# A cross attention in which TensorE takes the last three tiles of a unit in one step instead of two

## The chip, the cores and the metric

The kernel runs on one core of a Trainium2 chip. The metric is the time of one execution on the device, in microseconds (us). The kernel before took 3461.85 us, the median of three runs that lie between 3461.8 and 3472.22 us.

The core's engines each work through a program of their own and meet at semaphores: TensorE (PE in the profile, with its weight loads as PEld), VectorE (DVE), ScalarE (ACT), GpSimd (POOL) and SyncE (SP, which starts the DMAs).

## The reference, cut to what matters

The whole computation is a two-layer network over x (32 batches of 64 rows of 128) with a context of 32 x 1601 x 128: an attention with its feed-forward, a linear attention, a mixture of experts, a second cross attention, a rotary attention and a second mixture. The change touches the second cross attention alone:

```
def _L1_xattn_ref(x, context, mask, Wq, Wkv, Wout, b_out):
    HEADS = 16
    DIM_HEAD = 64
    SCALE = DIM_HEAD ** (-0.5)
    ...
    q = x @ Wq.T
    kv = context @ Wkv.T
    k, v = jnp.split(kv, 2, axis=-1)
    ...
    sim = jnp.einsum('bhid,bhjd->bhij', q, k) * SCALE
    max_neg = -jnp.finfo(sim.dtype).max
    sim = jnp.where(mask[:, None, None, :], sim, max_neg)
    attn = jax.nn.softmax(sim, axis=-1)
    out = jnp.einsum('bhij,bhjd->bhid', attn, v)
    out = out.transpose(0, 2, 1, 3).reshape(B, Nq, HEADS * DIM_HEAD)
    return out @ Wout.T + b_out
...
x = x + _L1_xattn_ref(_layernorm(x, axis=-1), ctx_1024, mask_BxS2_bf1, L1_xattn_Wq, L1_xattn_Wkv, L1_xattn_Wout, L1_xattn_b_out)
```

The kernel folds the weights: query and key weights of a head are one 128 x 128 matrix, and so are value and output weights. Scores are then folded queries against the raw context, and the probabilities mix the raw context before the folded value weights project it.

## The kernel before

The stage is `cross_attention_1` (from L2089). A unit `v` is half the heads (8) of one batch, 64 units in all, so a unit has 8 heads x 64 queries = 512 columns. Its context is cut into `KT` = 13 tiles of 128 rows (`kt` = 0 to 12). A tile `n` = 13 v + kt goes through these steps:

- `scores(n)` on PE (L2210): three bf16 matmuls 128x512 (L2221 to L2223) into one of three PSUM banks;
- `copy` on ACT (L2434) adds the mask and writes the scores to SBUF, `running_max` on DVE (L2336) follows it;
- `shift` on DVE (L2353) subtracts the maximum and `exp` on ACT (L2441) takes the exponential, both for two tiles at once, the last tile of a unit alone; POOL adds up the probabilities (L2179 to L2188);
- `mix(n)` on PE (L2241): context tile times probabilities, f32 128x512, which the chip runs as two MATMULs of L2248, accumulated over the 13 tiles of the unit.

`scores` runs `LEAD` = 22 tiles ahead of `mix`. Between them PE does small work, which `between(n)` (L2298) places by `kt`: `denominators` of the unit before at kt 1 (L2255), `project` at kt 3 (L2264), `turn_peaks` at kt 5 (L2229), `spread_shift` at kt 8 (L2237), `queries` and `final`.

- `queries` (L2268, matmuls at L2271) makes the folded queries of a later pair of batches, a quarter of the heads at a time. The table `QUERIES` = {(0, 10): 0, (1, 10): 1, (2, 9): 2, (2, 11): 3} gives the places as (v mod 4, kt); this runs while v // 4 + 1 < 16.
- `final` (L2274, matmul at L2277) stacks the result of a finished batch. It runs at kt 12 of every even unit after the first.

All of these small works write the same PSUM bank, `R_SMALL` = 7. `take_small` (L2204) makes each wait until the one before it has been read out: for `final` behind `queries` that is the semaphore `q_low`, and it is reached only when ACT has copied the bank (`queries` of act, L2448) and DVE has then subtracted (`queries` of dve, L2379). ACT and DVE have their place in their own programs for this, by the same (v mod 4, kt), behind the copy and the running maximum of tile n + 22.

The order of PE's work is written out by hand in the loop at L2313: for each unit, for each entry of `tile_pairs` (tiles 0-1, 2-3, 4-5, 6-7, 8-9, 10-11, and 12 alone), all `scores(n + 22)` of the step, then `between(n)` for each of its tiles, then all `mix(n)`. The loops of DVE (L2408) and ACT (L2462) go tile by tile and are not touched by the change.

Of the kernel before, what the change touches and what calls it, by code (L numbers as in the profile page):

```python
# [35 lines left out]
KT = -(-S // P)  # L36
# [2052 lines left out]
def cross_attention_1(c):  # L2089
# [51 lines left out]
    tile_pairs = [(j, 2 * j, min(2 * j + 2, KT)) for j in range(NP)]  # L2141
# [59 lines left out]
    def pe(eng):  # L2201
# [8 lines left out]
        def scores(n):  # L2210
            v, kt = n // KT, n % KT
            bt, b, half = v // 2, v // 2 % 2, v % 2
            if kt == 0:
                eng.wait_ge(q_low, bt // 2 * 4 + 2 * half + 2)
                eng.wait_ge(ctx_split, SPLIT * bt + SPLIT)
            wait_if(eng, copied, n - SB + 1)
            q = slice(half * QU, half * QU + QU)
            w = slice(kt * P, kt * P + P)
            o = c.ps[:, n % SB, 0:QU]
            i = bt // 2 % 2  # L2220
            eng.matmul(o, ch[:, b, w], qh[:, i, b, q], start=True, stop=False)  # L2221
            eng.matmul(o, ch[:, b, w], ql[:, i, b, q], start=False, stop=False)  # L2222
            eng.matmul(o, cl[:, b, w], qh[:, i, b, q], start=False, stop=True).then_inc(scored, 1)  # L2223
# [17 lines left out]
        def mix(n):  # L2241
            v, kt = n // KT, n % KT
            b = v // 2 % 2
            if kt == 0:
                eng.wait_ge(ctx_loaded[b], (v // 4 + 1) * 32)
                wait_if(eng, u_made, v - 1)
            eng.wait_ge(exps, v * NP + kt // 2 + 1)
            eng.matmul(c.ps[:, R_MIX + v % 2, :], ctxn[:, b, kt * D:(kt + 1) * D], st[:, v % 2, kt, :],  # L2248
                       start=kt == 0, stop=kt == KT - 1).then_inc(mixed, 1)
# [24 lines left out]
        def final(bt):  # L2274
            b = bt % 2
            take_small((out_made, bt + 1))
            mm = eng.matmul(c.ps[b * L:(b + 1) * L, R_SMALL, 0:D], c.C("stack"), acc[:, b, :], start=True, stop=True)  # L2277
            mm.then_inc(f_ps, 1)
# [19 lines left out]
        def between(n):  # L2298
            v, kt = n // KT, n % KT
            if kt == 1 and v > 0:  # L2300
                denominators(v - 1)
            if kt == 3 and v > 0:
                project(v - 1)
            if kt == 5 and v + 1 < UNITS:
                turn_peaks(v + 1)
            if kt == 8 and v + 1 < UNITS:
                spread_shift(v + 1)
            if (v % 4, kt) in QUERIES and v // 4 + 1 < PAIRS:
                queries(v // 4 + 1, QUERIES[v % 4, kt])
            if kt == 12 and v > 0 and v % 2 == 0:  # L2310
                final(v // 2 - 1)

        for v in range(UNITS + 1):  # L2313
            for j, a, z in tile_pairs:
                tiles = range(v * KT + a, v * KT + z)
                for n in tiles:
                    if n + LEAD < TILES:
                        scores(n + LEAD)
                for n in tiles:
                    between(n)  # L2320
                for n in tiles:
                    if n < TILES:
                        mix(n)
# [103 lines left out]
    def act(eng):  # L2427
# [34 lines left out]
        for n in range(TILES + KT):  # L2462
# [8 lines left out]
            if a < TILES and a % KT % 2 == 0:  # L2471
                exp(a // KT, a % KT // 2)

    m.engines = dict(sp=sp, pool=pool, pe=pe, dve=dve, act=act)
    m.after = [(out_made, B)]
    return m
# [482 lines left out]
```

## Time and profile before

| | |
|---|---|
| median of three runs | 3461.85 us |
| profiled execution, its time | 3466.28 us |
| its span, first to last instruction | 3464.4 us |
| outside the span | 1.88 us |
| granted TensorE clock, mean of the span | 0.967 |
| the stage of the change | about 1352 to 2905 us of the span |
| busy share of the span: PE, DVE, ACT, POOL | 95%, 69%, 55%, 46% |

The profile is one execution. A row of the timeline gives the start in us from the span's start, the duration, the engine, the line of the kernel, the operation with what it writes and reads, and in brackets the idle time of the engine ahead of it with what ended it. The recorded duration of a matmul includes a modelled end, so 0.38 us of a bf16 128x512 matmul is not its share of the stream: for that one reads the distance of starts. Rows that merge several instructions (x4) run to the end of the last. A few matmul records are missing from the trace (in the timeline a start is then skipped).

### The profile page before, as it was taken

To read this page: it belongs to the slowest core of one execution; us is meant where nothing else is said; L and a number is where in the kernel's file an instruction comes from. 1 tells how busy PE (TensorE), PEld (TensorE's weight loads), DVE (VectorE), ACT (ScalarE), POOL (GpSimd) and SP (SyncE) were. 2 spreads that over 40 slices of the span, in tenths; PEclk is the share of its full clock that TensorE was granted. 3 is DMA by queue.
4 is the path that set the end of the run, shared out by engine and by line. 5 is a ranking of instruction groups with operands and counts; after the bars stand their busy time and mean duration, and the time that the engine had idled before them with its cause. 6 is when DMAs were issued, how large, how long until landed. Compare 5 with 4: busy or idle time off the path is not lost. (4 is left out here: it accounts for less than half of the span.)

```text
span 3464.4 us, 67377 instructions
## 1 busy us (share of the span) xinstructions
PE 3283.1 (95%) x26253; PEld 1902.2 (55%) x26385; DVE 2391.5 (69%) x5437; ACT 1904.4 (55%) x2600; POOL 1609.5 (46%) x1271
## 2 busy tenths in 40 slices
PE   7799999999997898999999999999999997979998
PEld 4566666666665775455445555545554544655555
DVE  7877777777784435777777777777777775653333
ACT  5466666666664234666666666666666663432222
POOL 5433333333322102777777777777777764310000
PEclk7899999999999699999999999999999999979999
DMA  1133333333320002011110111101111000010000
GB/s 74 32 73 76 75 75 83 73 73 75 76 50 1 26 1 73 20 39 39 39 39 20 39 39 39 39 20 39 39 39 39 21 28 1 1 77 1 1 1 13
DMA packets 90493, 138.92 MB, mean 40 GB/s; under 512 B 14464, under 2 KB 67776, under 8 KB 89408
## 3 DMA queue, kind: packets, MB, share of 16 engines
q1 hardware_dynamic: 90176, 134.61, 14.3%
q8 instruction: 210, 3.44, 0.4%
q14 instruction: 107, 0.88, 0.1%
HBM read 94.15 MB, written 1.05 MB: 27 GB/s over the span
## 5 line engine op out<-in xcount | busy, mean ns | idle before, releaser
L2434 ACT ACTIVATE arena<-banks,arena 128x512 f32<-128x512 f32 x832 | 560.3, 687 | 477.4 <-PE banks L2223 477.4
L2248 PE MATMUL banks<-arena 128*128 128x512 f32 x1664 | 803.9, 603 | 0.8 <-ACT arena L2441 0.8
L2182 POOL TENSOR_TENSOR arena<-arena 128x1024 f32<-128x1024 f32 x256 | 603.9, 2359 | 165.7 <-ACT arena L2441 164.6
L1220 DVE TENSOR_REDUCE arena<-banks 128x1 f32<-128x512 f32 (+1 forms) x896 | 529.4, 627 | 166.6 <-PE banks L1056 162.3
L2336 DVE TENSOR_TENSOR banks<-arena,banks 128x512 f32<-128x512 f32 x640 | 444.2, 694 | 242.7 <-ACT arena L2434 223.1
L1357 ACT ACTIVATE arena<-banks 128x1024 f32<-128x1024 f32 (+1 forms) x448 | 423.7, 961 | 306.5 <-PE banks L1137 303.9
L2353 DVE TENSOR_TENSOR arena<-arena,banks 128x1024 f32<-128x1024 f32 (+1 forms) x448 | 507.1, 1133 | 1.6 <-PE banks L2238 1.2
L2441 ACT ACTIVATE arena<-arena 128x1024 f32<-128x1024 f32 (+1 forms) x448 | 443.0, 989 | 11.1 <-DVE arena L2353 10.9
L2248 PEld LDWEIGHTS banks<-arena 128*128 128x128 f32 x1664 | 290.0, 190 | 220.8 <-issue 200.1
L2223 PE MATMUL banks<-arena 128*128 128x512 bf16 x830 | 313.2, 377 | 2.5
L2222 PE MATMUL banks<-arena 128*128 128x512 bf16 x786 | 297.9, 379 | 4.1
L981 POOL TENSOR_TENSOR arena<-arena,one 128x512 bf16<-128x512 f32 x124 | 105.7, 852 | 400.5 <-ACT arena L1321 400.5
L1157 PE MATMUL banks<-arena 128*32 128x192 f32 (+1 forms) x6656 | 288.8, 279 | 2.2 <-ACT arena L1357 2.1
L2221 PE MATMUL banks<-arena 128*128 128x512 bf16 x754 | 285.4, 378 | 0.1
L1157 PEld LDWEIGHTS banks<-arena 128*32 128x32 f32 x6656 | 184.7, 109 | 154.0 <-ACT arena L1357 71.8
L2179 POOL TENSOR_TENSOR arena<-arena 128x1024 f32<-128x1024 f32 x64 | 151.3, 2365 | 229.6 <-ACT arena L2441 229.4
L2010 DVE SCALAR_TENSOR_TENSOR arena<-banks,weights,arena 128x512 f32<-128x512 f32 x128 | 95.9, 750 | 220.2 <-PE banks L1872 128.3
L1930 ACT ACTIVATE arena<-banks,weights 128x512 f32<-128x512 f32 x128 | 88.0, 687 | 260.8 <-PE banks L1862 260.8
L1056 PE MATMUL banks<-arena 64*128 64x512 bf16 x768 | 182.4, 383 | 31.2 <-DVE arena L1220 28.9
L1872 PEld LDWEIGHTS banks<-arena 128*128 128x128 f32 x1536 | 179.6, 193 | 44.8 <-issue 35.2
L1872 PE MATMUL banks<-arena 128*128 128x128 f32 x1536 | 186.6, 279 | 1.8 <-DVE arena L2010 1.7
L2222 PEld LDWEIGHTS banks<-arena 128*128 128x128 bf16 x832 | 81.1, 97 | 191.2 <-issue 144.1
(353 smaller groups left out, 5159.4 us busy)
## 6 DMA issues: line engine op xcount, KB each, us to landing
arena<-arena SPq DMA_DIRECT2D x768, 50.0 KB, 2.2
arena<-in_ctxT SPq DMA_DIRECT2D x32, 800.5 KB, 6.2
arena<-in_ctx SPq DMA_DIRECT2D x32, 768.0 KB
fold<-in_ctxT SPq DMA_DIRECT2D x16, 800.5 KB, 4.6
foldv<-in_ctxT SPq DMA_DIRECT2D x16, 800.5 KB, 5.0
arena<-in_m2w SPq DMA_DIRECT2D x3, 2048.0 KB, 13.3
arena<-in_xw SPq DMA_DIRECT2D x1, 2048.0 KB, 7.9
weights<-in_weights SPq DMA_DIRECT2D x1, 1920.0 KB, 12.3
```

Of the source, the lines that this page charges most:

```text
L1157: mm = eng.matmul(c.ps[HR * x:HR * x + HR, 6, a:z], v9[0:w, b, e:e + HR], pr[0:w, at % 4, rt * 512 + t2 * 256 + a:rt * 512 + t2 * 256 + z] ...
L1220: eng.tensor_reduce(o, s, AX, ALU.max).then_inc(a_max, 1)
L1357: eng.activation(pr[0:w, at % 4, :].rearrange("p (x n) -> p x n", x=2)[:, :, 0:n], c.ps[0:w, bank:bank + 2, 0:n], ACT.Exp, scale=scale).th ...
L1872: mm = eng.matmul(c.ps[:, 4 + e % 2, j * P:(j + 1) * P], hT[:, (g * units + u) % NH, j * P:(j + 1) * P], w3[:, wo * D:(wo + 1) * D], start ...
L2182: eng.tensor_tensor(part, part, tiles, ALU.add).then_inc(sums, 1)
L2222: eng.matmul(o, ch[:, b, w], ql[:, i, b, q], start=False, stop=False)
L2223: eng.matmul(o, cl[:, b, w], qh[:, i, b, q], start=False, stop=True).then_inc(scored, 1)
L2248: eng.matmul(c.ps[:, R_MIX + v % 2, :], ctxn[:, b, kt * D:(kt + 1) * D], st[:, v % 2, kt, :], start=kt == 0, stop=kt == KT - 1).then_inc(m ...
L2336: eng.tensor_tensor(peak if kt == KT - 1 else c.ps[:, R_MAX, :], st[:, v % 2, kt, :], so_far, ALU.max)\
L2353: eng.tensor_tensor(tiles, tiles, c.ps[:, R_SHIFT, :].unsqueeze(1).to_broadcast([P, z - a, QU]), ALU.subtract)\
L2434: eng.activation(st[:, v % 2, kt, :], c.ps[:, n % SB, :], ACT.Identity, bias=hide[:, kt, v // 2:v // 2 + 1])\
L2441: eng.activation(tiles, tiles, ACT.Exp, scale=scale).then_inc(exps, 1)
```

## The change

Tiles 10, 11 and 12 of a unit become one step of PE's loop. The steps up to tile 9 stay as they were. No instruction is added or taken away; the number of tiles in a step is all that changes, and with it the order in which PE issues the same work.

```diff
             if kt == 12 and v > 0 and v % 2 == 0:
                 final(v // 2 - 1)
 
+        steps = [(a, z) for _, a, z in tile_pairs[:-2]] + [(KT - 3, KT)]
         for v in range(UNITS + 1):
-            for j, a, z in tile_pairs:
+            for a, z in steps:
                 tiles = range(v * KT + a, v * KT + z)
                 for n in tiles:
                     if n + LEAD < TILES:
```

Written out, PE's order at the end of a unit is:

```
before: scores(10+22) scores(11+22)  between(10) between(11)  mix(10) mix(11)
        scores(12+22)  between(12)  mix(12)
after:  scores(10+22) scores(11+22) scores(12+22)
        between(10) between(11) between(12)  mix(10) mix(11) mix(12)
```

## Rows read from the trace of the kernel before

**Rows 1.** The page, busy time and its share of the span for each engine.
```profile
PE 3283.1 (95%) x26253; PEld 1902.2 (55%) x26385; DVE 2391.5 (69%) x5437; ACT 1904.4 (55%) x2600; POOL 1609.5 (46%) x1271
```

**Rows 2.** Busy us of each engine in two stretches of four units, granted clock (PEclk), DMA.
```profile
1400.00:1496.00 96.00, 95.52 (x432) 48.34 (x440) 74.38 (x115) 63.47 (x90) 71.14 (x45) 1.00 0.11 35
...
2739.00:2835.00 96.00, 95.57 (x434) 48.29 (x441) 74.20 (x115) 63.01 (x89) 69.33 (x43) 1.00 0.09 26
```

**Rows 3.** PE by line, 1400 to 2860 us: busy us, mean ns, then idle before.
```profile
L2248 PE MATMUL banks<-arena 128*128 128x512 f32 x1583 | 766.2, 603 | 0.0
```

**Rows 4.** Waits, 1400 to 2860 us: us in total, times, longest us.
```profile
ACT arena L2434 <- PE banks L2223: 465.3, 395, 2.0
...
PEld banks L2229 <- DVE arena L2373: 28.5, 61, 0.8
...
PEld banks L2277 <- DVE arena L2379: 6.4, 15, 0.4
PEld banks L2277 <- issue: 6.4, 15, 0.4
```

**Rows 5.** Timeline of PE, a step of two tiles without small work.
```profile
1821.05 0.38 PE L2221 MATMUL banks<-arena 128*128 128x512 bf16 x1
...
1822.34 1.88 PE L2248 MATMUL banks<-arena 128*128 128x512 f32 x4
1824.06 0.38 PE L2221 MATMUL banks<-arena 128*128 128x512 bf16 x1
```

**Rows 6.** Timeline of PE, tiles 10 to 12 of unit 18.
```profile
1828.46 0.38 PE L2221 MATMUL banks<-arena 128*128 128x512 bf16 x1
...
1829.76 1.05 PE L2271 MATMUL banks<-xT,fold 128*128 128x128 f32 x8
1830.65 1.88 PE L2248 MATMUL banks<-arena 128*128 128x512 f32 x4
1832.37 0.38 PE L2221 MATMUL banks<-arena 128*128 128x512 bf16 x1
...
1833.11 0.43 PE L2277 MATMUL banks<-arena,consts 128*64 128x128 f32 x2
...
1834.44 0.38 PE L2221 MATMUL banks<-arena 128*128 128x512 bf16 x1
```

**Rows 7.** Timeline of ACT and DVE, the same stretch of unit 18.
```profile
1831.41 0.60 ACT L2448 ACTIVATE arena<-banks 128x512 bf16<-128x512 f32 x1
...
1831.77 0.69 DVE L2336 TENSOR_TENSOR banks<-arena,banks 128x512 f32<-128x512 f32 x1
...
1832.37 0.68 DVE L2379 TENSOR_TENSOR arena<-banks,arena 128x512 bf16<-128x512 f32 x1
```

**Rows 8.** Timeline of PE, tiles 10 to 12 of unit 16.
```profile
1779.60 0.38 PE L2221 MATMUL banks<-arena 128*128 128x512 bf16 x1
...
1780.89 1.05 PE L2271 MATMUL banks<-xT,fold 128*128 128x128 f32 x8
...
1784.24 0.43 PE L2277 MATMUL banks<-arena,consts 128*64 128x128 f32 x2
...
1785.57 0.38 PE L2221 MATMUL banks<-arena 128*128 128x512 bf16 x1
```

**Rows 9.** Timeline of ACT and DVE, the same stretch of unit 16.
```profile
1781.98 0.60 ACT L2448 ACTIVATE arena<-banks 128x512 bf16<-128x512 f32 x1 [0.85 <-PE banks L2271]
...
1782.62 0.69 DVE L2379 TENSOR_TENSOR arena<-banks,arena 128x512 bf16<-128x512 f32 x1 [0.75 <-ACT arena L2448]
```

**Rows 10.** Busy us of each engine in stretches around lower clocks, granted clock as above.
```profile
1000.00:1050.00 50.00, 46.05 (x830) 30.20 (x818) 36.82 (x84) 30.01 (x36) 5.06 (x9) 0.97 0.14 27
...
2895.00:2898.00 3.00, 1.25 (x4) 0.28 (x2) 0.00 (x0) 0.60 (x1) 2.57 (x3) 1.00 0.00 0
...
2901.00:2904.00 3.00, 0.71 (x3) 0.34 (x3) 1.20 (x5) 0.00 (x0) 0.06 (x1) 0.58 0.00 0
```

**Rows 11.** Timeline of PE, at the end of the stage.
```profile
2897.94 1.02 PE L2255 MATMUL banks<-one,arena 128*128 128x1 f32 x8 [1.75 <-POOL arena L2188]
```

## The prediction

> **What bounds the kernel now.** Start with the busy shares of the page. PE is busy for 95% of the span and no other engine above 69% [rows 1]. Then take the stage of the change alone, by stretches of four units: in 96 us PE is busy for 95.5, at the full clock of 2.4 GHz (granted 1.00), DVE for 74 and ACT for 63 [rows 2]. The grouping by line says the same: ahead of 1583 matmuls of `mix` PE was idle for 0.0 us [rows 3]. The list of waits shows the others waiting for PE, ACT for 465.3 us before its copies [rows 4]. So in this stage time is PE's stream: work of PE that is only reordered costs nothing, and every us in which PE stands still is a us of the kernel, since no later slack of PE can take it back.
>
> The distance of starts gives the stream's prices. In a step of two tiles without small work, six score matmuls take 1822.34 - 1821.05 = 1.29 us, so one tile of scores 0.645, and four MATMULs of `mix` take 1824.06 - 1822.34 = 1.72 us, 0.86 a tile [rows 5].
>
> **What the change takes away.** One alternation between scores (bf16) and mixes (f32) per unit, 64 in all. I take its price as nothing: the step of rows 5 is 3.01 us for two tiles, and a single-tile step at the same rates would be 1.505 us. Nothing in that step is left over for a turn. The largest turn I can find is at small work: `final` starts 0.31 us after the last score matmul (1832.80 from the even spacing behind 1832.37, then 1833.11) where 0.215 is the spacing [rows 6]. Charged to all 64 units, 0.1 us would be 6 us of gain. That is one end; the other is zero, and rows 5 are the nearer case, because the alternation that goes is one without small work.
>
> **What it moves.** The three scores of a step need three free banks. Scores of tile 12 + 22 wait for the copy of tile 9 + 22, issued a step earlier; 1.72 us of mixes and 1.29 us of scores lie between. ACT's copy takes less than 0.7 us, and ACT is the one who waits [rows 4]. Cost nothing. Mixes of tiles 10 to 12 need exponentials that ACT makes before its copy of tile 10 + 22, or right behind tile 9's. Cost nothing. The next unit's scores start 2.58 us of mixes behind the last ones; again the copies are done. No DMA and nothing of POOL's program is touched or passed.
>
> The small work is another matter. `queries` and `final` use one bank, and `final` waits until ACT and DVE have emptied it. Before, two mixes and one tile of scores lay between them: 1.72 + 0.645 = 2.36 us of PE's own work. After, nothing lies between them where both fall into tiles 10 to 12. Behind the waiting `final` on PE stand the mixes of 10, 11 and 12 and everything after; they are ready and can't pass. The table of places gives two such cases.
>
> Case A, `queries` at kt 11 (v mod 4 = 2, v = 2 to 58): 15 times. In unit 18 the last query matmul ends at 1829.76 + 1.05 = 1830.81, ACT's copy runs from 1831.41 to 1832.01, DVE's running maximum to 1832.46, DVE's subtraction from 1832.37 to 1833.05, and `final` starts at 1833.11, 0.06 us later [rows 6, 7]. The whole cover is used up already: the waits name L2379 as what was last before 15 of the 30 `final`s, though the 0.4 us there are no longer than at the 15 that name only issue, so nothing is lost yet [rows 4]. After the change queries end 0.645 later, at 1831.46, so ACT can copy from 1831.50 to 1832.10; DVE was busy until 1832.46 with its running maximum in either order, so the subtraction stays where it is and `final` starts at 1833.11 as before. But PE has by then not done mixes 10 and 11. Everything after is late by just those: 1.72 us. 15 x 1.72 = 25.8 us.
>
> Case B, `queries` at kt 10 (v mod 4 = 0, v = 4 to 56; unit 0 has no `final`): 14 times. In unit 16 queries end at 1780.89 + 1.05 = 1781.94; ACT starts its copy at 1781.98, 0.04 later, and DVE ends at 1782.62 + 0.69 = 1783.31 [rows 8, 9]. Both engines waited for this, so the chain moves with it: 0.645 later, to 1783.95, and `final` starts at 1784.01 instead of 1784.24. It comes 0.23 us earlier with 1.72 us of mixes still to do: 1.72 - 0.23 = 1.49 us late. 14 x 1.49 = 20.9 us.
>
> The other units: v mod 4 = 1 has `queries` at kt 10 and no `final`; v mod 4 = 3 has neither; units 60 and 62 have a `final` and no `queries`. Cost nothing, with one doubt. In v mod 4 = 1 ACT and DVE get their query work 0.645 us later and do what is queued behind it later (exponential, copies, shift, running maxima). `turn_peaks` of the next unit already waits for DVE's projection (28.5 us over 61 times, 0.47 on average against the 0.42 that a turn shows at `final`, longest 0.8) [rows 4]. If the lag reached it, it could cost up to 0.8 - 0.47 = 0.3 us in 16 units, 5 us. DVE has over 20 us of idle in 96 to take it up [rows 2], so I take zero.
>
> **The sum.** 25.8 + 20.9 = 46.7 us longer. Against the profiled execution: span 3464.4 + 46.7 = 3511.1, with the 1.88 us outside it 3513.0 for an execution that took 3466.28. The median lies 4.43 us below that execution, so 3461.85 + 46.7 = 3508.5 us.
>
> **A rule against a row: the clock.** While the clock is granted in full here, PE will now stand still for up to 1.8 us at a time, 29 times. The trace has such a gap at the end of this stage: PE was idle for 1.75 us after dense mixes [rows 11], with 1.25 of 3 us busy, and the granted clock of that stretch stayed at 1.00; it fell to 0.58 (part of it at 1.2 GHz) only in 2901 to 2904, after small matmuls and a second gap, with 0.71 of 3 us busy [rows 10]. In the new gaps dense work stands directly on both sides. I take no loss. The Trainium skill ("TensorE: Matmul & The Clock Gate", the section "Why this matters for your kernels") warns that idle gaps between bursts of matmuls send the clock back to its lower level. By that rule the time is that of rival 1; the trace agrees with it for the second gap, not for the first.
>
> The Trainium skill ("Perfetto Trace Analysis", section "Matmul Optimizations") also asks that matmuls execute back-to-back in batches, which would speak for larger steps. The stretches of this stage are at 1.00 already [rows 2], so by this trace a larger batch has nothing to win.
>
> **The rivals.**
> 1. The stalls are there and the clock falls in many of them. In the stretch 1000 to 1050 the clock fell once, and the mean of 0.97 makes that (1 - 0.97) x 50 = 1.5 us [rows 10]. In all 29 stalls that is 44 us, 3552; in half of them 3530. Against it speak rows 10 and 11. Chance 0.07.
> 2. Faster: the alternation has a price that starts don't show, and the bank is free sooner than I say, because DVE takes the query work ahead of its other work. This decides if the stalls together stay under 6 us, 0.2 us each. Then 3461.85 - 6 + 0 to 6 = 3456 to 3462. Against it: DVE's order is fixed, and with nothing queued ahead the chain from the last query matmul to the end of L2379 is still 1.36 us [rows 8, 9]. Chance 0.02.
> 3. The stalls are longer than the chain, or a second wait follows them. In case B ACT has, behind the query copy, an exponential and the copies of tiles 11 + 22 and 12 + 22 still to do, which before were partly done by then. After the stall PE has 3 x 0.86 us of mixes and 0.645 of scores ahead of the first scores that need the second of these copies, 3.2 us, against some 0.7 + 1.0 + 0.7 us on ACT. Should 0.5 us be missing each time, it is 29 x 0.5 = 14.5 us more, 3523. Chance 0.05.
> 4. The change does nothing, since PE does other work in the wait. There is none: PE's order is fixed. Chance 0.01.
>
> **How the numbers follow.** The forecast, stalls of case A and B at full clock, has 0.85, at 3508.5. Its own bounds are - 6 (alternations) and + 5 (lag at `turn_peaks`), and about 4 us either way for the spread of the medians: 3498.5 to 3517.5. To hold 8 in 10 nothing more is needed, but a few falls of the clock (5 x 1.5) belong in: 3498 to 3524. A measurement of this kernel can tell about 0.3%, 10.4 us, from no change. Faster 0.02 (rival 2 in part), same 0.03, slower 0.95.
>
> **What would show each step right or wrong.** In the profile after, L2277 (one line lower) should show an idle time of some 1.6 to 2.1 us before it, ended by L2379's counterpart, in 29 places, together near 50 us; PE's busy time in a stretch of four units stays 95.5 while the stretch takes 99.2 us instead of 96.0 (two stalls). The granted clock stays 1.00 there. `mix` and scores show no other waits. Wrong if the idle time ahead of `final` is well under 1.3 us, if the clock falls behind it, or if waits appear at `scores`, `mix` or `turn_peaks`.

## The result and the profile after

The changed kernel takes 3517.43 us, the median of four runs (3509.99 to 3524.8), against 3467.03 us for four runs of the kernel before beside it: a ratio of 1.0143, 95% interval 1.0114 to 1.0172. Its profiled execution has a span of 3511.5 us, where the kernel before had 3464.4. Line numbers behind the change are one higher (ACT's copy is L2435, its query copy L2449, DVE's running maximum L2337, its subtraction L2380); on PE `mix` stays L2248, `queries` L2271, `final` L2277.

The page of the kernel after, engines:

```profile
PE 3297.0 (94%) x26385; PEld 1908.2 (54%) x26385; DVE 2393.3 (68%) x5437; ACT 1901.7 (54%) x2600; POOL 1611.7 (46%) x1271
```

Busy us of each engine over four units, twice, granted clock, DMA (answers to [rows 2]):

```profile
1500.00:1599.20 99.20, 96.14 (x441) 48.60 (x441) 74.31 (x114) 62.81 (x89) 70.63 (x44) 1.00 0.11 34
1699.00:1798.20 99.20, 96.14 (x441) 48.54 (x440) 74.36 (x115) 62.82 (x89) 70.64 (x44) 1.00 0.11 34
```

Every engine does the work it did, in a longer time. (PE's busy time is 0.6 us above [rows 2] because this trace has all 441 matmul records and that one 432.) The clock is still granted in full. Four units take 99.15 us instead of 95.96; this measure, used below, is the distance between the starts of the first `mix` of a unit and of the unit four later. Unit by unit it is 25.76 instead of 24.27, 23.71 as before, 26.88 instead of 25.16, and 22.82 as before. From the first to the last MATMUL of `mix` the stage takes 1561.3 us (1377.6 to 2938.9) instead of 1514.8 (1380.8 to 2895.6): 46.5 of the 47.1 us by which the spans differ lie inside it.

Waits of the kernel after, 1400 to 2905 us, total us, times, longest (answers to [rows 4]):

```profile
ACT arena L2435 <- PE banks L2223: 497.3, 350, 3.4
...
PEld banks L2277 <- DVE arena L2380: 50.0, 29, 1.8
PE banks L2277 <- DVE arena L2380: 44.5, 29, 1.6
...
PEld banks L2229 <- DVE arena L2374: 28.6, 61, 0.8
...
PEld banks L2277 <- issue: 0.4, 1, 0.4
```

The one new row that matters is the third of those shown: PE idle for 44.5 us ahead of `final`, 29 times, ended by the queries' subtraction. In [rows 4] PE itself had no such row.

Timeline of PE at a kt-11 place (answers to [rows 6]):

```profile
1840.01 1.05 PE L2271 MATMUL banks<-xT,fold 128*128 128x128 f32 x8
1842.70 0.43 PE L2277 MATMUL banks<-arena,consts 128*64 128x128 f32 x2 [1.64 <-DVE arena L2380]
1843.07 2.84 PE L2248 MATMUL banks<-arena 128*128 128x512 f32 x6
1845.75 0.38 PE L2221 MATMUL banks<-arena 128*128 128x512 bf16 x1
```

ACT there, then DVE (answers to [rows 7]):

```profile
1841.10 0.60 ACT L2449 ACTIVATE arena<-banks 128x512 bf16<-128x512 f32 x1
```

```profile
1840.24 1.21 DVE L2354 TENSOR_TENSOR arena<-arena,banks 128x1024 f32<-128x1024 f32 x1
1841.37 0.69 DVE L2337 TENSOR_TENSOR banks<-arena,banks 128x512 f32<-128x512 f32 x1
1841.97 0.68 DVE L2380 TENSOR_TENSOR arena<-banks,arena 128x512 bf16<-128x512 f32 x1
```

The last query matmul ends at 1841.06 and ACT's copy at 1841.70, DVE is busy with its running maximum until 1842.06, its subtraction ends at 1842.65 and `final` starts 0.05 us later. Six MATMULs of `mix` (x6) stand behind it; four of them used to be ahead.

Timeline of PE at a kt-10 place, then DVE (answers to [rows 8, 9]):

```profile
1792.12 0.43 PE L2277 MATMUL banks<-arena,consts 128*64 128x128 f32 x2 [1.41 <-DVE arena L2380]
1792.48 2.84 PE L2248 MATMUL banks<-arena 128*128 128x512 f32 x6
```

```profile
1791.37 0.69 DVE L2380 TENSOR_TENSOR arena<-banks,arena 128x512 bf16<-128x512 f32 x1 [1.40 <-ACT arena L2449]
```

Here DVE had been idle for 1.40 us: nothing but the chain itself holds the bank.

### The profile page after: what moved, and what is told of

The parts are those of the page before. It is cut to its first block and busy times, and to the rows that moved or that the text cites. A ratio compares the mean times of both kernels' runs of the same rounds, so it can differ in the third digit from the quotient of the medians.

```text
span 3511.5 us, 67509 instructions
## 1 busy us (share of the span) xinstructions
PE 3297.0 (94%) x26385; PEld 1908.2 (54%) x26385; DVE 2393.3 (68%) x5437; ACT 1901.7 (54%) x2600; POOL 1611.7 (46%) x1271
## 5 line engine op out<-in xcount | busy, mean ns | idle before, releaser
L2435 ACT ACTIVATE arena<-banks,arena 128x512 f32<-128x512 f32 x832 | 555.9, 688 | 507.7 <-PE banks L2223 507.7
L2248 PE MATMUL banks<-arena 128*128 128x512 f32 x1664 | 793.8, 603 | 0.8 <-ACT arena L2442 0.8
L2337 DVE TENSOR_TENSOR banks<-arena,banks 128x512 f32<-128x512 f32 x640 | 444.6, 695 | 267.5 <-ACT arena L2435 247.2
L2248 PEld LDWEIGHTS banks<-arena 128*128 128x128 f32 x1664 | 292.2, 190 | 245.6 <-issue 230.7
L2222 PE MATMUL banks<-arena 128*128 128x512 bf16 x832 | 315.3, 379 | 0.0
L2221 PE MATMUL banks<-arena 128*128 128x512 bf16 x832 | 314.9, 378 | 0.0
L2223 PE MATMUL banks<-arena 128*128 128x512 bf16 x832 | 314.0, 377 | 0.0
```

Source lines behind the costliest of these rows:

```text
L2337: eng.tensor_tensor(peak if kt == KT - 1 else c.ps[:, R_MAX, :], st[:, v % 2, kt, :], so_far, ALU.max)\
L2435: eng.activation(st[:, v % 2, kt, :], c.ps[:, n % SB, :], ACT.Identity, bias=hide[:, kt, v // 2:v // 2 + 1])\
```

## The experiments

The theory: all of the loss is `final` standing right behind `queries` on one bank, 1.72 us fifteen times and 1.49 us fourteen times; the merge of the steps is free. The rivals: the step of three tiles costs by itself; the alternation that goes is worth something; the clock falls in the stalls.

### Merged step, queries moved away from final

```diff
-    QUERIES = {(0, 10): 0, (1, 10): 1, (2, 9): 2, (2, 11): 3}
+    QUERIES = {(0, 9): 0, (1, 10): 1, (2, 7): 2, (2, 9): 3}
```

> The merged step of tiles 10 to 12 as in the changed kernel, but the queries leave it wherever a final follows: the table of places becomes {(0, 9): 0, (1, 10): 1, (2, 7): 2, (2, 9): 3}. Theory (the loss is the two small works meeting on one bank without cover): no idle of TensorE ahead of L2277, four units take 96.0 us as before the change, the kernel is equal to the one before within 3 us (ratio 1.000). Rival (the step of three tiles costs by itself, by its three scores in a row or by a lag of ScalarE and VectorE): four units stay near 99.2 us and the kernel stays 47 us above. Rival (the alternation that the merge saves is worth 0.1 us a unit): four units take 95.6 us, 6 us faster than before.

Measured: 3466.87 us against 3468.86 us before, ratio 0.9994 (0.9985 to 1.0002). Four units take 95.95 us. Its waits, 1400 to 2860 us:

```profile
PEld banks L2277 <- issue: 12.7, 30, 0.4
```

PE itself has no wait ahead of L2277 in that list. The whole loss goes once other work stands between the two small works, and the step of three tiles stays. Together with the next run this answers the first two rivals.

### The same places without the merge

The partner of the last one: the kernel before with that table of places alone.

> The kernel before, its steps of two tiles and one kept, with only the table of the queries' places changed to {(0, 9): 0, (1, 10): 1, (2, 7): 2, (2, 9): 3}. It is the partner of the merged kernel with that table: the two differ in the merge alone. Theory (the merge by itself is worth nothing): four units take 95.96 us here as there, equal to before within 3 us. Rival (moving the queries gains what the merge loses, or the reverse): four units differ from 95.96 here.

Measured: 3469.82 us against 3470.1 us, ratio 1.0002 (0.9992 to 1.0012), four units 95.95 us. The pair differs in the merge alone, and the merge is worth 0.00 us in four units.

### Two steps kept, final moved next to queries

```diff
-            if kt == 12 and v > 0 and v % 2 == 0:
+            if kt == 11 and v > 0 and v % 2 == 0:
                 final(v // 2 - 1)
```

> The two steps of the kernel before are kept (tiles 10 and 11, then 12); only the final moves on TensorE from kt 12 to kt 11, so it stands right behind the queries and ahead of the mixes of 10 and 11. VectorE's order is untouched. Theory: the loss comes without any merge. At kt 11 (15 times) final starts when L2379 ends, as before, and everything behind it is late by two mixes and one tile of scores, 1.72 + 0.645 = 2.36 us; at kt 10 (14 times) the chain starts where it did, final is 0.87 us earlier with 2.36 us of work still to do, 1.49 us late. 15 x 2.36 + 14 x 1.49 = 56 us slower than before, four units 99.85 us. Rival (the merged step is what costs): equal to before.

Measured: 3541.59 us, ratio 1.0207 (1.0193 to 1.0221), 73 us above before where 56 was expected. The sign and the place are right, so the loss comes without any merge. Four units take 99.80 us in half of the groups, as the theory has it (99.85), and 101.49 us in the other half. PE's timeline at a slow one:

```profile
1548.07 1.05 PE L2271 MATMUL banks<-xT,fold 128*128 128x128 f32 x8
1551.41 0.43 PE L2277 MATMUL banks<-arena,consts 128*64 128x128 f32 x2 [2.29 <-DVE arena L2379]
1551.77 3.31 PE L2248 MATMUL banks<-arena 128*128 128x512 f32 x4
1554.87 0.64 PE L2221 MATMUL banks<-arena 128*128 128x512 bf16 x1
1555.29 0.59 PE L2222 MATMUL banks<-arena 128*128 128x512 bf16 x1
1555.72 0.38 PE L2223 MATMUL banks<-arena 128*128 128x512 bf16 x1
```

Busy time and granted clock of the same kernel there:

```profile
1548.00:1551.00 3.00, 1.12 (x10) 0.90 (x8) 2.66 (x4) 2.32 (x4) 1.77 (x2) 1.00 0.01 3
1551.00:1554.00 3.00, 2.59 (x5) 1.17 (x6) 0.35 (x1) 0.00 (x0) 0.00 (x0) 0.72 0.00 0
```

Four MATMULs of `mix`, 1.72 us at 2.4 GHz, take 3.10 us from start to start here, and the first scores come 0.43 us apart instead of 0.215: that is 1.2 GHz. Behind seven of the fifteen stalls of 2.29 us the granted clock fell, each time 0.7 to 1.03 us after the stall's end, and each fall cost 101.49 - 99.80 = 1.69 us, 12 us in all. The falls are no scatter: they stand behind every second stall. The sum 56 + 12 = 68 us is what the stage shows: its `mix` runs from 1383.1 to 2965.9, 1582.8 us instead of 1514.8. The other 9 of the 77 us by which this span (3541.6) is above that of the kernel before lie outside the stage.

### Merged step, final behind the mix of tile 11

```diff
                 for n in tiles:
+                    if n % KT == 12 and v > 0 and v % 2 == 0:
+                        final(v // 2 - 1)
                     if n < TILES:
                         mix(n)
```

> The merged step as in the changed kernel, queries where they are, but TensorE takes final between the mix of tile 11 and the mix of tile 12 of the same step. The cover of two mixes, 1.72 us, is back; the tile of scores (0.645 us) is not, since it stands ahead of the queries. Theory: the chain behind the queries takes 1.64 us from TensorE's last query start spacing to final at kt 11 and 1.41 at kt 10, both under 1.72, so nothing is lost at either: equal to before within 3 us, four units 96.0 to 96.2 us. Rival (three tiles of scores in a row are the loss): stays 47 us above before.

Measured: 3470.39 us, ratio 1.0007 (0.9998 to 1.0017), four units 96.06 us, 0.10 more than before. Two mixes of cover are enough for both chains. PE's timeline at the kt-10 place:

```profile
1780.65 1.88 PE L2248 MATMUL banks<-arena 128*128 128x512 f32 x4
1782.46 0.43 PE L2277 MATMUL banks<-arena,consts 128*64 128x128 f32 x2
...
1785.08 1.05 PE L2255 MATMUL banks<-one,arena 128*128 128x1 f32 x8
1786.00 1.10 PE L2248 MATMUL banks<-arena 128*128 128x512 f32 x2
```

From the first of four MATMULs to `final` it is 1.81 us where the four take 1.72. So `final`, which uses half of the array's columns (128*64), starts 0.09 us late behind an f32 matmul as it does behind a bf16 one, where it is 0.31 instead of 0.215 [rows 6]: this is no price of the alternation between types, and as the kernel before pays the same, it is not the 0.10 us either.

The 0.10 us lies one small work further on. `denominators` (L2255) takes the bank behind `final`, and it takes 0.92 us to the next `mix` here, where the kernel before takes 0.80:

```profile
1786.87 0.95 PE L2255 MATMUL banks<-one,arena 128*128 128x1 f32 x8
1787.67 1.10 PE L2248 MATMUL banks<-arena 128*128 128x512 f32 x2
```

The list of waits has a row for it that the kernel before lacks, with 14 entries, as many as there are kt-10 places:

```profile
PEld banks L2255 <- DVE x L2387: 4.7, 14, 0.3
```

DVE reads `final`'s result until 1785.02 here, 0.06 us ahead of `denominators`; in the kernel before it is done 0.71 us ahead (1786.16, then 1786.87). It is the same mechanism with another pair of small works.

### Only one of the two cases left

The merged kernel with the queries' places of case A moved ({(0, 10): 0, (1, 10): 1, (2, 7): 2, (2, 9): 3}), so that case B is left:

> The changed kernel with the queries of v mod 4 = 2 moved from kt 9 and 11 to kt 7 and 9; those of kt 10 stay, so only case B is left. Theory (the two cases add): the idle time before L2277 stands in 14 places at 1.41 us and in none at 1.65; four units take 95.96 + 1.49 = 97.45 us, the kernel is 20.9 us above before (ratio 1.006). Rival (the loss hangs on the merged step as a whole, through a lag that both share): a different split, four units not at 97.45.

And with those of case B moved ({(0, 9): 0, (1, 10): 1, (2, 9): 2, (2, 11): 3}), so that case A is left:

> The changed kernel with the queries of v mod 4 = 0 moved from kt 10 to kt 9; those of kt 9 and 11 stay, so only case A is left. Theory: 15 places with 1.65 us of idle time before L2277, four units 95.96 + 1.72 = 97.68 us, the kernel 25.8 us above before (ratio 1.0074). Rival as in the kernel with case B alone.

Measured, case B alone: 3486.73 us against 3466.6 us, ratio 1.0062 (1.0042 to 1.0083), four units 97.44 us, + 1.48. Case A alone: 3496.68 us, ratio 1.0084 (1.0065 to 1.0103), four units 97.67 us, + 1.71. The two add to 3.19; the changed kernel has 99.15 - 95.96 = 3.19. The median of case A alone is 30 us above before where 25.8 were expected; its stage is 25.8 us longer, as expected (`mix` from 1384.7 to 2925.3), and the rest is inside the interval of the ratio. PE's waits with case B alone:

```profile
PE banks L2277 <- DVE arena L2380: 19.8, 14, 1.4
```

and with case A alone:

```profile
PE banks L2277 <- DVE arena L2380: 24.7, 15, 1.6
```

### Merged step, VectorE takes the queries first

```diff
+            early = kt == 11 and (v % 4, kt) in QUERIES and v // 4 + 1 < PAIRS
+            if early:
+                queries(v // 4 + 1, QUERIES[v % 4, kt])
             if n + LEAD < TILES:
                 running_max(n + LEAD)
```

(and not again in its old place)

> The changed kernel; only VectorE's order differs: at kt 11 it takes the queries' subtraction ahead of the running maximum of tile 11 + 22. Theory (in case A it was VectorE's own queue, not the chain, that held the bank): the subtraction starts 0.03 us after ScalarE's copy, as at kt 10, the 15 idle times fall from 1.65 to about 1.41 us, four units from 99.15 to 98.91 us, 3.6 us in all. Rival (the length in case A is set by ScalarE's queue): 1.65 stays.

Measured: four units 98.92 us, 0.23 less than the changed kernel, and PE's waits:

```profile
PE banks L2277 <- DVE arena L2380: 41.0, 29, 1.4
```

All 29 stalls are now 1.41 us. So at kt 11 the bank was held by what DVE had queued ahead. The 3.5 us can't be told in the times (3515.02 us here, 3513.67 and 3517.43 us for the changed kernel); the trace alone shows them.

### Two steps, final next to queries, VectorE takes the queries first

The kernel before with TensorE's `final` at kt 11 and with the order of VectorE of the last experiment.

> As the kernel with two steps and final at kt 11 on TensorE, with VectorE's subtraction at kt 11 ahead of its running maximum. There the idle time of 2.29 us at kt 11 was followed by a stretch at a lower granted clock in seven of fifteen cases, which took the loss from the 56 us of the theory to about 70. Theory (the length of the idle time decides): it falls by 0.2 to 0.35 us to about 2.0; the loss without the clock is then 51 to 53 us, and the falls of the clock get fewer or vanish, so the kernel is 51 to 60 us above before. Rival (ScalarE's queue sets the length): 2.29 stays, seven falls stay, 70 us above before.

Measured: 3529.57 us, ratio 1.0178 (1.0156 to 1.0201), 63 us above before, 3 us outside the 51 to 60 expected. The kt-11 stalls are 1.98 us; the clock fell behind five of the fifteen, where it fell behind seven of them at 2.29. Four units take 99.49 us without a fall, 3.53 more than before, so 15 places at 2.05 and 14 at 1.49 make 52 us, and 5 x 1.69 = 8 us more come from the clock; together 60, which is what the stage shows (`mix` from 1383.6 to 2958.4). The stall at kt 11 got shorter, from 2.29 to 1.98 us, so DVE's queue had a share in it here too, as the theory had it. That a shorter stall brings fewer falls is not shown by this: the falls again keep a rhythm, behind every third or fourth of the fifteen stalls here and behind every second one before, and no run shows what picks the stalls out. Nor has any run a stall between 1.65 and 1.98 us among dense matmuls.

### The changed kernel again

> The changed kernel once more, on the same chip as the three others, for the size of the loss beside them and for the granted clock of each run. Theory: 46.7 us above before, the clock of its runs as high as that of the kernels without the stalls. Rival (the stalls sometimes bring the clock down): some of its runs show a mean clock 0.005 or more below the others and are 10 us or more longer, which the kernels without the stalls don't show.

Measured: 3513.67 us (3509.39 to 3515.73), 1.0126 (1.0113 to 1.014), 44.8 us above before. Mean clocks of its four runs are 0.965 to 0.967, those of 21 runs of the kernel before beside it 0.964 to 0.969. In three profiles with 1.65 us stalls (the changed kernel twice, case A alone) no fall follows any of the 45. In the first set of runs, though, one run of 3524.8 us had a mean clock of 0.960 and one of 3521.49 us 0.962; the kernel before, beside all the experiments, went down to 0.961 as well (a run of 3478.47 us). So did kernels without a stall of 1.65 us: case B alone has a run of 3496.34 us at 0.960, and a kernel without any stall at `final` (tiles 4 and 5 split, below) one of 3486.09 us at 0.961. A low mean is no sign of these stalls, then; but the two low runs of the changed kernel have no trace, so whether a stall of 1.65 us now and then brings the clock down stays open.

### Tile by tile: doubling the alternations

The table of places as in the first experiment, and

```diff
-            for j, a, z in tile_pairs:
+            for a, z in [(t, t + 1) for t in range(KT)]:
```

> As the kernel before with the queries' places {(0, 9): 0, (1, 10): 1, (2, 7): 2, (2, 9): 3}, and TensorE goes tile by tile: 13 alternations between scores and mixes in a unit instead of 7. Theory (an alternation costs nothing): 95.96 us for four units where no wait appears. Rival (it costs up to 0.1 us): 24 alternations more in four units, up to 98.4 us, 38 us slower in all. The small work keeps its places, so its cover of scores and mixes between two users of the bank is partly shorter; a wait that comes of that would show as idle time at the small works' lines and is counted apart.

Measured: 3516.94 us against 3470.1 us, ratio 1.013 (1.0107 to 1.0153), four units 98.99 us, + 3.03. It looks like the rival, but PE's waits name another cause:

```profile
PE banks L2237 <- DVE arena L2353: 43.5, 59, 0.8
```

The timeline shows `spread_shift` (L2237) starting 1.12 us behind the last score matmul on average, where 0.215 is the spacing: 0.90 us a unit, 3.6 in four. From scores to `mix` the distance is 0.215 us, from `mix` to scores 0.43, as inside a type; 24 more alternations cost nothing. And the sum is short by 0.6: `turn_peaks` (L2229) starts 0.215 us behind the scores here, against 0.34 before. That is a wait of the kernel before which the prediction had taken for a fixed cost.

### Splitting the step of turn_peaks, and turn_peaks between two mixes

Tiles 4 and 5 as two steps, the rest as before:

> The kernel before with its step of tiles 4 and 5 taken as two steps of one tile, queries and final where they were. In the kernel before turn_peaks at kt 5 starts 0.34 us after the last score matmul, against 0.215 us in the kernel that goes tile by tile: the bank it takes is held by VectorE's projection, the same kind of wait as in the changed kernel, 0.13 us in every unit. Splitting the step puts one mix (0.86 us) ahead of it. Theory (an alternation costs nothing and cover on the shared bank is all that counts): that wait goes, four units take 95.96 - 0.5 = 95.45 us, the kernel is 8 us faster than before (ratio 0.9977), 55 us faster than the changed one. Rival (a step of single tiles has a cost of its own): no gain or a loss.

Measured: 3479.59 us, ratio 1.0031 (1.0019 to 1.0043), four units 96.61 us, + 0.65: a miss. The wait at `turn_peaks` went, and a new one came three tiles later, PE's waits:

```profile
PE banks L2237 <- DVE arena L2353: 11.1, 60, 0.2
```

DVE of this kernel ahead of its maxima:

```profile
1824.27 0.70 DVE L2336 TENSOR_TENSOR banks<-arena 128x512 f32<-128x512 f32 x1 [1.71 <-ACT arena L2434]
1824.88 0.69 DVE L2341 TENSOR_REDUCE banks<-banks 128x4 f32<-128x512 f32 x1
```

It was idle for 1.71 us for the scores of tile 5 + 22, which now come behind a mix, and so, as I read it, it was late for the shift that `spread_shift` waits for. Hence the last one, which keeps the scores early and moves only `turn_peaks`:

```diff
-            if kt == 5 and v + 1 < UNITS:
-                turn_peaks(v + 1)
...
                 for n in tiles:
+                    if n % KT == 5 and v + 1 < UNITS:
+                        turn_peaks(v + 1)
                     if n < TILES:
                         mix(n)
```

> The kernel before with its steps as they were; TensorE takes turn_peaks between the mix of tile 4 and the mix of tile 5 instead of ahead of both. In the kernel with tiles 4 and 5 in two steps the wait at turn_peaks went (0.18 us a unit with its slower transposes) but spread_shift at kt 8 then waited 0.35 us a unit for VectorE, which had got the scores of tile 5 + 22 later and stood idle for 1.71 us for them ahead of its maxima. Here those scores stay early and only turn_peaks is 0.86 us later. Theory (cover on what a small work waits for decides, at both ends): turn_peaks finds its bank free, VectorE starts its reduction some 0.9 us earlier than there, spread_shift doesn't wait: four units take 95.96 - 0.73 = 95.23 us, the kernel is 12 us faster than before (ratio 0.9966). Rival (the wait moves to spread_shift whatever is done, since VectorE is the one that is full there): four units 95.9 to 96.6, no gain or a loss.

Measured: 3453.59 us against 3464.34 us, ratio 0.9966 (0.9953 to 0.9979), four units 95.23 us. It is faster than both kernels. PE's timeline at that place:

```profile
1816.37 1.02 PE L2248 MATMUL banks<-arena 128*128 128x512 f32 x2
1817.22 0.60 PE L2229 MATMUL banks<-consts,arena 128*128 128x128 f32 x4
1817.66 1.02 PE L2248 MATMUL banks<-arena 128*128 128x512 f32 x2
```

`turn_peaks` starts 0.85 us behind the first of two MATMULs, with nothing left over for a wait, and its four transposes take 0.44 us to the next start.

## Why the prediction was right

The forecast was 3508.5 us with 3498 to 3524 for the range, by + 46.7 us. Spans differ by 3511.5 - 3464.4 = 47.1 us. The ratios of the two sets of runs, 1.0143 and 1.0126, lie on both sides of the 1.0135 that 46.7 us make. The stage by itself is 46.5 us longer. The first median, 3517.4, is 9 us above the forecast, 5 us of it because the kernel before was at 3467.0 in that set, not at 3461.85.

- **PE's stream is the time of the stage.** Right: the stalls are found in the time one to one, and no later slack took anything back. Units without a stall took what they did, to 0.01 us.
- **The alternation costs nothing.** Right, by the pair with and without the merge (95.95 and 95.95) and by 24 more alternations. The reason given for it was short of one step: the 3.01 us of a step contain its turns, so halving them can't show that a turn is free. It is the spacing inside each type that does, since 6 x 0.215 and 4 x 0.43 make all of the 3.01. The 0.1 us at `final`, which I charged to a turn between types as the upper bound, belongs to the half-width matmul; as a bound it did no harm.
- **Case A, 1.72 us.** Measured 1.72 (25.16 to 26.88), alone 1.71. That DVE's own queue, and not the chain alone, sets it was shown by letting DVE take the queries first: the price fell by 0.23 us.
- **Case B, 1.49 us.** Measured 1.49 (24.27 to 25.76), alone 1.48.
- **Nothing else waits.** Right for scores, mixes and copies. The lag at `turn_peaks`, the doubt of 5 us, did not come: its waits are 28.6 us in 61 against 28.5 [rows 4].
- **The floor at `turn_peaks`.** Wrong in a side step. I set its 0.47 us of weight-load wait against the 0.42 at `final` and read 0.05 of wait. The 0.42 is the half-width matmul's; `turn_peaks` uses the full array and can start at the spacing of 0.215. It was waiting 0.13 us, its transposes ran slower too, and removing both gave 0.73 us in four units. It changed nothing in the sum, since the change did not touch it.
- **The clock, rival 1.** Right for this kernel, but the row that it rested on was in part luck. The witness was the gap of 1.75 us at the end of the stage, behind which the clock stayed full [rows 10, 11]. The changed kernel has the same gap there, and in its trace the clock fell 0.9 us after the gap's end:

```profile
2941.22 1.02 PE L2255 MATMUL banks<-one,arena 128*128 128x1 f32 x8 [1.75 <-POOL arena L2188]
2942.51 1.98 PE L2264 MATMUL banks<-foldv,arena 128*64 128x128 f32 x16 [0.28 <-DVE arena L2360]
```

  Busy time and granted clock there:

```profile
2939.00:2942.00 3.00, 1.25 (x10) 0.81 (x8) 0.00 (x0) 0.60 (x1) 1.99 (x2) 1.00 0.00 0
2942.00:2944.00 2.00, 1.73 (x17) 1.64 (x18) 0.18 (x1) 0.00 (x0) 0.00 (x0) 0.53 0.00 0
```

  In the kernel before, the same 16 matmuls of L2264 took 1.10 us. The gap stands in 13 traces of this case with 1.74 to 1.78 us, and in four of them the clock fell within 1.1 us of its end. So one trace with a full clock did not prove such a gap harmless. What shows it for the new stalls are the 45 places at 1.65 us. At 1.98 and 2.29 us, with two tiles of scores ahead instead of three and two mixes behind instead of three, the clock fell in five and seven of fifteen cases. The Trainium skill ("TensorE: Matmul & The Clock Gate", section "Why this matters for your kernels") warns of idle gaps between bursts, but of longer ones than any of these. So the prediction read more into the page than it says, where it had the time of rival 1 follow from its rule. Nor does the page fit the runs: 1.98 us was enough in five places, and the measurement decides. My estimate from the five falls at 1.98 us: had the change put the stall 0.3 us longer, the forecast would have been some 8 us too low.
- **The signs named ahead.** The idle time before `final` was to be 1.6 to 2.1 us and near 50 us together; it is 1.65 and 1.41, the second below what was named, and 44.5 us together, since the idle time counts from the modelled end of the last matmul and I had counted case A from the start it could have had. The places (29), who ends it, 99.2 us for four units and the clock of 1.00 were as named.

## What to carry to other kernels

On an engine that is full and takes its work in order, a small piece that shares a buffer with the piece before it needs as much other work between the two as the buffer's emptying takes, here 1.41 to 1.65 us over two other engines. Before steps are regrouped, list which small works fall into one step and measure that chain from the last matmul to the release; what was ahead of the wait and is now behind it is the loss. When such a wait is removed by moving a piece, look at what the next engine was fed by the old order, or the wait comes back one piece later, as it did at `spread_shift` (0.65 us in four units) and at `denominators` (0.10 us).

## What the runs showed of the hardware

- Alternating between bf16 and f32 matmuls of full width is free: 0.215 and 0.43 us between starts across the change of type as within it.
- A matmul with 64 of 128 columns (128*64) starts 0.09 us late behind a full-width one of either type: 0.31 us instead of 0.215 behind bf16, 1.81 instead of 1.72 behind four f32 MATMULs.
- With TensorE dense on both sides, an idle time of 1.65 us left the granted clock at 1.00 in 45 of 45 places; at 1.98 us it fell in 5 of 15 and at 2.29 us in 7 of 15, for 1.69 us of loss each, in a rhythm (behind every third or fourth of these stalls, and behind every second one). With small matmuls behind it, a gap of 1.75 us was followed by a fall within 1.1 us in 4 of 13 traces.
